# Starting a mixture of experts from seven of ten row tiles: six full expert tiles ahead of the last row tile

## What is computed

```python
x = x + _L0_gnn_ref(_layernorm(x), batch0, edge_index, W)      # attention over edges, 8 heads of 64
x = x + _L0_ffn_ref(_layernorm(x)[None], ...)[0]               # 8 experts, 2 for each node
x = x + _L1_gnn_ref(_layernorm(x), ..., src, dst)              # aggregate, project, layernorm, gelu
x = x + _L1_ffn_ref(_layernorm(x)[None], ...)[0]               # 6 experts, 1 for each node

# _L0_ffn_ref, for a node xf and its two best experts by xf @ gate_w:
h1 = rmsnorm(gelu(xf @ w1[e]), n1[e])
h2 = rmsnorm(gelu(h1 @ w2[e]), n2[e])
out = sum over the two of softmax(logit) * ((h2 + h1) @ w3[e])
```

## Time and profile before

| | us |
|---|---|
| median of 3 runs (lowest, highest) | 937.22 (934.82, 939.62) |
| the profiled execution's own time | 939.32 |
| its span in the trace | 937.6 |
| TensorE busy, share of the span | 842.7, 90% |
| VectorE busy | 572.0, 61% |
| ScalarE busy | 367.8, 39% |
| GpSimd busy | 221.4, 24% |

### The profile page before, as it was taken

How to read it: one execution, slowest core, us unless ns; L and a number is a source line. 1 busy time by engine, 2 the same in 40 slices (tenths; PEclk the granted TensorE clock), 3 DMA queues, 4 the chain that set the end, 5 groups by cost and what they waited for, 6 DMA issues and landing times.

```text
span 937.6 us, 15975 instructions
## 1 busy us (share of the span) xinstructions
PE 842.7 (90%) x5064; PEld 568.4 (61%) x5064; DVE 572.0 (61%) x1871; ACT 367.8 (39%) x674; POOL 221.4 (24%) x425
## 2 busy tenths in 40 slices
PE   6999999999999999999996399999829999983996
PEld 3456565367777777777775277777514444862674
DVE  6489999267778878887773245555524509674121
ACT  1234444366666566656662133434200021331331
POOL 4100000000012201220122322222156404773443
PEclk9999999999999999999998599999959999975999
DMA  9817867894011322014109545553123540254450
GB/s 251 305 39 203 203 194 197 188 302 119 28 51 51 100 59 77 24 50 179 53 24 326 161 121 156 157 171 105 61 83 89 128 144 27 102 187 102 152 178 27
DMA packets 86980, 121.27 MB, mean 129 GB/s; under 512 B 40270, under 2 KB 49646, under 8 KB 86638
## 3 DMA queue, kind: packets, MB, share of 16 engines
q1 hardware_dynamic: 73293, 102.08, 37.3%
q0 software_dynamic: 13600, 18.11, 6.7%
HBM read 65.78 MB, written 57.08 MB: 131 GB/s over the span
## 4 chain that ended last, share of the span: by engine, by line
PE 75%; DVE 11%; issue 5%; DMA 4%; ACT 2%; POOL 2%; SPq 0%; DVEq 0%; POOLq 0%; ACTq 0%
PE ps L715 18%; PE ps L608 10%; PE ps L637 10%; PE ps L779 9%; PE ps L619 8%; PE ps L498 4%; PE ps L804 4%; PE ps L722 4%; DVE R_B L1547 3%; DVE R_B L1546 2%; PE ps L503 2%; DVE R_A L1648 1%; PE ps L448 1%; PE ps L674 1%; DVE R_B L1542 1%
## 5 line engine op out<-in xcount | busy, mean ns | idle before, releaser
L715 PE MATMUL ps<-R_B,R_A 128*128 x612 | 187.4, 448 | 3.0 <-ACT R_A L1181 1.1
L715 PEld LDWEIGHTS ps<-R_B,R_A 128*128 128x128 f32 x612 | 112.9, 196 | 35.3 <-issue 24.8
L1026 ACT ACTIVATE R_A<-R_A,neg_max 125x1250 f32<-125x1250 f32 x80 | 106.6, 1333 | 56.6 <-DVE neg_max L1648 56.6
L1648 DVE CUSTOM_DVE_ANT_0 R_A<-ps,R_B,neg_max 125x417 f32<-125x417 f32 (+1 forms) x160 | 97.6, 648 | 29.0 <-PE ps L608 29.0
L608 PE MATMUL ps<-R_B 64*125 64x417 f32 (+1 forms) x480 | 106.5, 544 | 1.6 <-ACT XN L968 1.5
L637 PEld LDWEIGHTS ps<-R_W,XN 125*64 125x64 f32 x1600 | 85.3, 136 | 23.9 <-issue 23.8
L619 PE MATMUL ps<-ident,R_A 125*125 125x125 f32 x800 | 98.6, 278 | 0.0
L619 PEld LDWEIGHTS ps<-ident,R_A 125*125 125x125 f32 x800 | 94.9, 188 | 1.5 <-DVE R_W L1655 0.7
L637 PE MATMUL ps<-R_W,XN 125*64 125x125 f32 x1600 | 94.7, 272 | 0.8 <-DVE counted L1702 0.8
L1033 ACT ACTIVATE R_W<-ps 125x500 f32<-125x500 f32 x120 | 66.1, 585 | 51.1 <-PE ps L619 51.1
L1547 DVE TENSOR_SCALAR R_B<-R_B 125x418 bf16<-125x418 uint16 x200 | 76.8, 384 | 0.0
(11 more groups left out here) (238 smaller groups left out, 1134.8 us busy)
## 6 DMA issues: line engine op xcount, KB each, us to landing
slots_d<-R_B SPq DMA_DIRECT2D x9, 2322.0 KB, 12.1
R_B<-in_L_ffn_w_dram SPq DMA_DIRECT2D x28, 512.0 KB, 6.9
R_A<-slots_d SPq DMA_DIRECT2D x27, 256.0 KB, 2.9
slots_d<-R_A SPq DMA_DIRECT2D x27, 256.0 KB, 2.3
counts_d<-R_A SPq DMA_DIRECT2D x10, 546.9 KB
logs_d<-R_B SPq DMA_DIRECT2D x10, 546.9 KB
R_B<-logs_d SPq DMA_DIRECT2D x10, 546.9 KB
R_B<-counts_d SPq DMA_DIRECT2D x10, 546.9 KB
```

What stands on the lines that cost most here:

```text
L715: ins = pe.matmul(bank(b, TM, width), lhs[:, c * TM:c * TM + TM], flat[:, bass.ds(e * (n * width) + c * width, width)], start=c == 0, stop ...
L1026: act.activation(SC[u % 2][h], SC[u % 2][h], ACT.Exp, bias=neg_max[:, 2 * (u % 2) + h:2 * (u % 2) + h + 1], scale=-1.0, accum_out=den[:, 2 ...
L1648: dve.tensor_tensor_reduce(SC[u % 2][h][:, a:z], bank(2 * h + g % 2, P, z - a), LNB[i % 2][:, a:z], -1.0, least if t else 3.0e38, ALU.add, ...
```

## The change

The first six expert tiles (EARLY_TILES) are taken from the full tiles that the first seven row tiles (EARLY_ROWS) already fill; there are always six. Their counts are taken out at u = 36 (take_out_counts), and DVE works out owners and bases of these six tiles at the ends of u = 36, 37 and 38 (early_counts, early_owners, early_done; early_owners gives the first slot_made). SP loads the rows of tiles 0 to 2 when unit 38's weights are turned. The weights and norm vectors are loaded one by one, as attention lets go of the buffer beneath each; for that the queries lie by row tile, and XR and the routing's small tiles have moved. TensorE ends its attention loop at u = 40, and the output turn of unit 39 and the turn, logits and ranks of row tile 9 are written out by hand between the steps of tiles 0 to 3; the same on ACT, DVE and POOL. The counts of all rows are then taken out behind first_product(3). DVE makes of them the rest: rest_counts before second_squares(2) (the second slot_made with its first operation, for which third_product(1) waits), rest_owners in step 4 behind second_norm(2), rest_bases behind first_norm(4) (the third slot_made). SP waits for the third slot_made and all scatters before it loads the rows of tile 5, and turn_tile(6) and first_squares(6) wait for it too. The reloads of step 3 and later move four steps on. The gates come after the expert loop, and POOL's inverse degrees behind the root of row tile 8.

```diff
+EARLY_TILES, EARLY_ROWS = 6, 7
+assert K0 * P * EARLY_ROWS - E0 * (TM - 1) > (EARLY_TILES - 1) * TM
...
-        QT = R_B[:, 0:5000].rearrange("p (j n) -> p j n", j=4)
+        QT = R_B[:, 0:5000].rearrange("p (i j n) -> p i j n", i=T, j=4)
...
-        XR = [R_A[0:P, 5000 + WIDE * k:5000 + WIDE * k + WIDE] for k in range(3)]
+        XR = [R_B[0:P, 13056:13056 + WIDE], R_W[0:P, 5250:5250 + WIDE], R_B[0:P, 13572:13572 + WIDE]]
```

On SyncE:

```diff
-            sp.wait_ge(S("s_made"), 6 * UNITS)
...
-            sp.wait_ge(S("z_made"), 6 * UNITS)
...
-            sp.wait_ge(S("o_made"), UNITS)
...
+            for e in range(3):
+                load_w1e(e)
+            load_logs(9)
+            sp.wait_ge(S("s_made"), 6 * 9 * PAIRS)
+            load_w1e(3)
+            sp.wait_ge(S("z_made"), 6 * 9 * PAIRS)
+            load_w2e(4)
+            load_w2e(5)
+            sp.wait_ge(S("s_made"), 6 * (9 * PAIRS + 1))
+            load_w1e(5)
+            sp.wait_ge(S("s_made"), 6 * (9 * PAIRS + 2))
+            load_w1e(6)
+            sp.wait_ge(S("s_made"), 6 * (9 * PAIRS + 3))
+            load_w1e(7)
+            load_w2e(0)
             sp.wait_ge(S("slot_made"), 1)
             for k in range(3):
-                sp.wait_ge(rows_out[k], 16 * K0 * len(range(k, T, 3)))
+                sp.wait_ge(rows_out[k], 16 * K0 * len(range(k, EARLY_ROWS, 3)))
+            sp.wait_ge(S("p_turned"), BLOCKS * (UNITS - 1))
+            for t in range(3):
+                load_rows0(t)
+            sp.wait_ge(S("s_made"), 6 * UNITS)
+            load_w1e(4)
+            sp.wait_ge(S("o_made"), UNITS - 1)
+            load_norm(L0_ffn_n1, N1B, S("nrm_in"))
+            sp.wait_ge(S("z_made"), 6 * UNITS)
+            for e in (1, 2, 3, 6, 7):
+                load_w2e(e)
+            sp.wait_ge(S("o_made"), UNITS)
+            load_norm(L0_ffn_n2, N2B, S("gam_in"))
...
-            for t in range(MT0 + 2):
+            for t in range(3, MT0 + 2):
+                if t == EARLY_TILES - 1:
+                    sp.wait_ge(S("slot_made"), 3)
+                    for k in range(3):
+                        sp.wait_ge(rows_out[k], 16 * K0 * len(range(k, T, 3)))
                 if t < MT0:
                     load_rows0(t)
```

On TensorE (in the attention loop, the wait of a product, and behind the loop):

```diff
+            def take_out_counts(k):
+
+                pe.matmul(bank(7, 1, 8, 144), ident[0:126, 125:126], counted[:, k, :], start=True, stop=True,
+                          skip_group_check=True).then_inc(S("count_made"), 1)
...
-            for u in range(UNITS - PAIRS + RANKS_AT + 1):
+            for u in range(UNITS + 1):
...
+                    if tile_at(u, RANKS_AT) == EARLY_ROWS:
+                        take_out_counts(EARLY_ROWS % 2)
...
             def third_product(t):
+                if t == 1:
+                    pe.wait_ge(S("slot_made"), 2)
...
             turn_tile(0)
+            turn_output(UNITS - 1)
+            first_product(0)
+            turn_tile(1)
+            turn_first(0)
+            first_product(1)
+            turn_normed_row(T - 1)
+            turn_tile(2)
+            second_product(0)
+            output_bank_free(UNITS)
+            route_tile(T - 1)
+            turn_first(1)
+            first_product(2)
+            turn_second(0)
+            turn_tile(3)
+            rank_tile(T - 1)
+            second_product(1)
+            third_product(0)
+            turn_first(2)
+            first_product(3)
+            pe.wait_ge(S("rank_taken"), T)
+            take_out_counts(T % 2)
+            turn_second(1)
+            turn_tile(4)
+            second_product(2)
+            third_product(1)
+            for t in range(4, MT0 + 2):
```

On ScalarE:

```diff
-            act.wait_ge(S("gate_step"), 1)
-            act.activation(gates[:, 0, :], gates[:, 0, :], ACT.Exp).then_inc(S("gate_exp"), 1)
...
             move_tile(0)
...
+            first_gelu(0)
+            move_tile(1)
+            move_first(0)
+            first_gelu(1)
+            move_normed_row(T - 1)
+            move_tile(2)
+            second_gelu(0)
+            for t in range(2, MT0 + 2):
...
+            act.wait_ge(S("gate_step"), 1)
+            act.activation(gates[:, 0, :], gates[:, 0, :], ACT.Exp).then_inc(S("gate_exp"), 1)
```

On GpSimd:

```diff
+            for i in range(T - 1):
                 rstd_tile(S("ln_stat"), T + i + 1, i, None, S("ln_rstd"))
+                if i == T - 2:
+                    inverse_degrees()
                 masks_of(i)
                 slots_for(i)
...
+            inverse_rms(0, S("ss_made"), 1, S("rms_made"))
+            inverse_rms(0, S("ss_made"), 2, S("rms_made"))
+            inverse_rms(1, S("ss2_made"), 1, S("rms2_made"))
+            masks_of(T - 1)
+            inverse_rms(0, S("ss_made"), 3, S("rms_made"))
+            inverse_rms(1, S("ss2_made"), 2, S("rms2_made"))
+            slots_for(T - 1)
+            pool.wait_ge(S("count_made"), 2)
```

On VectorE, the bookkeeping and its places (early_counts at the end of step 36, early_owners of 37, early_done of 38):

```diff
+            def early_counts():
+                link(dve.tensor_scalar(cnt_i[0:1, :], cnt_i[0:1, :], 7, None, ALU.logical_shift_right))
+                link(dve.tensor_copy(full, cnt_i[0:1, :]))
+                link(dve.scalar_tensor_tensor(filled, iota8[0:1, :], -float(CAP // TM), full, ALU.mult, ALU.add))
+                link(dve.tensor_tensor_scan(ahead, ones_row, filled, 0.0, ALU.mult, ALU.add))
+                link(dve.tensor_scalar(step_of, filled, -1.0, float(CAP // TM), ALU.mult, ALU.add))
+            def early_owners():
+                tiles = EARLY_TILES
+                of, first = owner_f[:, 0:tiles], base_f[:, 0:tiles]
+                link(dve.tensor_tensor(early_owner, iotaT[:, 0:tiles].unsqueeze(2).to_broadcast([1, tiles, 8]),
+                                       cnt[0:1, 2:3, :].to_broadcast([1, tiles, 8]), ALU.is_ge))
+                link(dve.tensor_reduce(of, early_owner, X_AXIS, ALU.add))
+                link(dve.tensor_copy(owner_i[:, 0:tiles], of))
+                link(dve.tensor_tensor(early_owner, early_owner, cnt[0:1, 3:4, :].to_broadcast([1, tiles, 8]), ALU.mult))
+                link(dve.tensor_reduce(first, early_owner, X_AXIS, ALU.add))
+                link(dve.tensor_tensor(first, first, iotaT[:, 0:tiles], ALU.add))
+                dve.tensor_scalar(base_i[:, 0:tiles], first, float(TM), None, ALU.mult).then_inc(S("slot_made"), 1)
+            def early_done():
+                link(dve.tensor_scalar(ahead, ahead, float(EARLY_TILES), None, ALU.min))
+                link(dve.tensor_copy(taken[:, 0:1], ahead[:, 0:1]))
+                link(dve.tensor_tensor(taken[:, 1:8], ahead[:, 1:8], ahead[:, 0:7], ALU.subtract))
+            def rest_counts():
+                dve.wait_ge(S("count_made"), 2)
+                dve.tensor_scalar(cnt_i[0:1, :], bank(7, 1, 8, 144), float(TM - 1), None, ALU.add)\
+                   .then_inc(S("slot_made"), 1)
+                dve.wait_ge(S("slot_made"), 2)
+                link(dve.tensor_scalar(cnt_i[0:1, :], cnt_i[0:1, :], 7, None, ALU.logical_shift_right))
+                link(dve.tensor_copy(full, cnt_i[0:1, :]))
+                link(dve.scalar_tensor_tensor(filled, iota8[0:1, :], -float(CAP // TM), full, ALU.mult, ALU.add))
+                link(dve.tensor_scalar(step_of, filled, -1.0, float(CAP // TM), ALU.mult, ALU.add))
+                link(dve.tensor_tensor(filled, filled, taken, ALU.subtract))
+                link(dve.tensor_tensor_scan(ahead, ones_row, filled, 0.0, ALU.mult, ALU.add))
+                link(dve.tensor_tensor(step_of[:, 0:7], step_of[:, 0:7], taken[:, 1:8], ALU.add))
+            rest = MT0 - EARLY_TILES
+            rest_owner, rest_of = owner[:, 0:rest, :], owner_f[:, EARLY_TILES:MT0]
+            rest_first = base_f[:, EARLY_TILES:MT0]
+            def rest_owners():
+                link(dve.tensor_tensor(rest_owner, iotaT[:, 0:rest].unsqueeze(2).to_broadcast([1, rest, 8]),
+                                       cnt[0:1, 2:3, :].to_broadcast([1, rest, 8]), ALU.is_ge))
+                link(dve.tensor_reduce(rest_of, rest_owner, X_AXIS, ALU.add))
+                link(dve.tensor_scalar(rest_of, rest_of, float(E0 - 1), None, ALU.min))
+                link(dve.tensor_copy(owner_i[:, EARLY_TILES:MT0], rest_of))
+            def rest_bases():
+                link(dve.tensor_tensor(rest_owner, rest_owner, cnt[0:1, 3:4, :].to_broadcast([1, rest, 8]), ALU.mult))
+                link(dve.tensor_reduce(rest_first, rest_owner, X_AXIS, ALU.add))
+                link(dve.scalar_tensor_tensor(rest_first, iotaT[:, 0:rest], taken[:, 0:1], rest_first, ALU.add, ALU.add))
+                dve.tensor_scalar(base_i[:, EARLY_TILES:MT0], rest_first, float(TM), None, ALU.mult)\
+                   .then_inc(S("slot_made"), 1)
...
+            first_squares(0)
+            first_norm(0)
+            first_squares(1)
+            first_norm(1)
+            second_squares(0)
+            take_logits(T - 1)
+            pick_two(T - 1)
+            second_norm(0)
+            first_squares(2)
+            first_norm(2)
+            second_squares(1)
+            take_ranks(T - 1)
```

(17 more changed lines are left out.)

134 lines of the change are left out of this document (74 added, 60 removed).

## The result

The changed kernel takes 924.78 us (median of 4 runs, 924.32 to 925.81); the kernel before, beside it, 938.25 (4 runs, 934.82 to 939.62). The ratio is 0.9863 with a 95% interval of 0.9834 to 0.9893, which lies wholly under 1, so it is faster, by 13.5 us, where 11.1 had been forecast (926.1, range 918 to 932). The profiled execution took 924.32 us and its span is 922.5.

The account below looks back on a forecast made before the run. TensorE bounds the kernel, with a 23.5 us gap of hardly any work between attention and experts. Tile 5 turned 13.7 us earlier, less 2.55 for the low clock, gives 11.1 off 937.2: 926.1 us, range 918 to 932.

Parts of the forecast that it names:

- a new stall: TensorE idle 7.8 us before tile 5, whose load awaits bases and scatters; turned 35.75 after attention's last product ends (zero).
- the one for the first count operation: TensorE idle 1.95 us before third product 1, as POOL's scatters delay tile 3's root and so DVE's count.
- Attention: Early count on TensorE and sixteen tiny DVE operations in units 36 to 38 lengthen attention by 1.05 us.
- the low clock behind the stall: After 7.8 idle us before tile 5, the next 5.1 us do half their work: 2.55 us lost.
- The norm vectors: Loads asked for at -4.1 and later, first needed at 5.4 and 12; costed at nothing, upper bound 2.4 us late.
- The two added table loads: Exp between two uses of Gelu on ACT adds two loads of 1.28 us, covered by waits; nothing lost.
- Weights loaded early go out on an otherwise quiet queue: SP's early weight loads during attention cost nothing, since only later loads are queued behind SP's waits.
- no-stall: Rival: tile 5 turned at 27.95 without a long wait, clock held; gain 21.5 us, 915.7; chance 0.07 for the whole.
- The early fall of the clock: Rival: clock falls in the 2.05 us idle before tile 0's norm, costing half of 5.1 us: 928.7; shared chance 0.22.
- late vectors: Rival: norm vectors land late and cost 2.4 us, 928.5; 931 with an early clock fall; shared chance 0.22.
- The slower rival: Clock stays low from 5.9 through the filled stretch; tile 5 comes 18 us later, 944; chance 0.04.
- the price that the prediction put on them: By the skill's HAM section, the two small stalls before tile 5 would each cost 2.5 us more, giving 931.

Follow-up runs that it names:

- the second experiment: Changed kernel with tile 3's inverse root put first on POOL, ahead of row tile 9's slots and two scatters: 924.32 us, ratio 0.9858 to the kernel before.
- the filled wait: Changed kernel with 32 extra matmuls that nobody reads ahead of tile 5's turn on TensorE: 924.63 us, ratio 0.9854 to the kernel before.
- the late owners: Changed kernel with the early tiles' owner operations at the end of unit 38 instead of 37: 926.5 us, ratio 0.9858 to the kernel before.
- the count first: Changed kernel with DVE's eight count operations ahead of tile 3's norm instead of behind it: 925.96 us, ratio 0.9858 to the kernel before.
- the edits together: Changed kernel with SP's wait at tile 6, owners in unit 38, counts before tile 3's norm, and remaining owners and bases earlier: 917.47 us, ratio 0.976.
- The third experiment: Changed kernel with all eight first-weight loads moved back behind the last scores: 931.31 us, ratio 0.9935 to the kernel before.
- the wait at tile 6: Changed kernel with SP's wait for remaining bases and scatters one tile later, ahead of tile 6's load: 918.48 us, ratio 0.9797 to the kernel before.

## Why the prediction was right

**Where the time came from.** As forecast, the gap between attention and experts filled with the first tiles, and a new stall stood in front of tile 5. The tile came at zero + 35.37; forecast were 35.75. The wait there was 7.65 us (7.8), the one for the first count operation 2.42 (1.95), the one for tile 0's norm 2.13 (2.05). The chain over VectorE, GpSimd and SyncE, each link priced from a row of the kernel before, held to 0.65 us in every place, and the second experiment bears out the link that was least plain, the inverse root behind the scatters. Some of the closeness is luck, for misses cancelled. TensorE's stretch of queued work began at zero + 6.49 (5.9 forecast) but took 12.80 us up to the count and not 13.75; the last base came at zero + 31.47 (32.1), but from there to tile 5's turn it took 3.90 us and not 3.65.

**Attention.** 1.05 us was the cost forecast. The ranks that stand in unit 36 begin at 472.38 in the changed kernel and at 473.18 in the kernel before, and zero is 505.25 and 505.18, so the stretch grew from 32.00 to 32.87: 0.87 us. Of that 0.65 is the wait in unit 38 (0.81 us, formerly 0.16), which moving the owners took away. The early count itself is 0.20. The changed kernel, and then the one before, TensorE in order of time:

```profile
472.38 0.39 PE L719 MATMUL ps<-counted,before 126*126 126x8 f32 x2
```

```profile
473.18 0.39 PE L681 MATMUL ps<-counted,before 126*126 126x8 f32 x2
```

**The clock.** 2.55 us were forecast for the low clock behind the stall; the experts ended 2.08 later than tile 5's lead would have them, and the filled wait gives 2.10. The term was half a microsecond too high, because the clock was back 4.2 us after work resumed and not 5.1.

**The total.** 11.1 us were forecast; the medians differ by 13.5, the profiled executions by 15.0 (939.32 and 924.32). In the profiles tile 5 is 15.04 earlier, where the forecast had 13.7. Of these 1.4 us, 0.38 come from the shorter chain, 0.18 from attention's cost and 0.80 from an attention that started earlier in that execution, which the change has no part in. With the clock's 2.08 the experts end 12.96 us earlier. The other 2.1 of the profiles' 15 us lie in the stages behind them, from the last third product's start to the end of the span (256.5 us, not 258.65), and such a difference also exists between executions whose later stages are alike: in the nine profiles of the changed kernel and its variants it is 256.4 to 258.6 us, with a mean of 257.25. That is 1.4 under the one profile of the kernel before, which is not enough to say whether the change shortens these stages. Between the medians of the two kernels, what is left over the forecast is 2.4 us, with an interval of the ratio that is itself 5.5 us wide; it is not settled beyond that.

**What was costed at nothing.** The norm vectors were asked for at 501.2 and 505.8. The second landed 8.4 us later, at 514.2; the trace has no landing of the first, which took 7.1 us with the late owners, 4.8 with the count first and 7.6 with the edits together. TensorE's wait for tile 0's norm was 2.13 us, and VectorE's norm itself began behind GpSimd's root; the forecast's 2.05 has no late vector in it. The two added table loads on ScalarE take 1.28 us each and are covered: TensorE's wait ahead of the aggregation is 16.92 us, 17.51 before, and behind the second of the loads (757.30) ScalarE still waits 5.67 us for VectorE. ScalarE in order of time at the first of the two:

```profile
665.87 1.28 ACT L1188 ACT_TABLE_LOAD   x1
667.16 0.21 ACT L1188 ACTIVATE gates<-gates 125x10 f32<-125x10 f32 x1
```

The load begins 0.02 us behind the activation ahead of it (665.47 + 0.38), and the exponential 0.01 us behind the load. The Trainium skill, page "ScalarE: Activation LUTs", section on what ACT_TABLE_LOAD costs, makes about 2.7 us of 1.28 for the load and 1.38 for a drain. The load agrees; no gap of 1.38 us stands on either side of it here, and the measurement decides.

**Where it was too short.** "Weights loaded early go out on an otherwise quiet queue" counted as a cost of nothing, and the sum began with the first product unhindered. It does not say that without them the first product would stand. The third experiment shows 6.8 us resting on it. The forecast came out since the weights were there, but a reader would have taken the gain for that of order alone.

**The rivals.** The stall is real, so no-stall is out as a forecast; as an experiment, one line takes it away, and 918.48 stands against the 915.7 reckoned for it. Of that, 0.97 us are left in front of tile 6, and the fall of the clock behind the count's wait made the chain 0.9 longer; the rest was not taken apart. The early fall of the clock was given 0.22 together with late vectors. It did not happen in the changed kernel's profile, but did in four of the profiles of its variants: behind the count's wait in three (the wait at tile 6, the filled wait, the late owners), in the first products in one (the count first). Behind the count it cost less than the 2.6 us reckoned. The wait for the bases took up what TensorE alone lost, and what was left is what the chain grew by: from the first count operation to the last base 9.04, 9.09 and 9.08 us in these three, 8.18 in the changed kernel. The slower rival, the clock low through the whole filled stretch, is excluded here by 1.00 from 505 to 537. It is real in a kernel that lets the clock fall first: with row tile 9 put first it was at 0.50 from 512 to 528, and the gain was down to 0.2%. The Trainium skill, "TensorE: Matmul & The Clock Gate", section on HAM oscillation, has bursts of matmuls start slow each time behind a long DMA wait. This case agrees: each of the six waits of 6.7 to 7.8 us in front of tile 5 was followed by work at 0.50. The section's case does not hold waits near 2 us, so the price that the prediction put on them does not follow from it. Here such waits went either way.

## What to carry to other kernels

When work is moved ahead into a gap, ask what it then waits for: here a single wait stood one tile ahead of where the data required it, and moving that line gave 6 us on top of the 13.5 of the whole rework. Ask too what the old order let happen in good time: weights loaded early carried half of this gain. Follow the small operations of the side engines link by link, since those, and not the big matmuls, set when the next load may go. Judge small edits in front of a long wait by what they do to the chain that ends it, for the wait swallows all that only the waiting engine gains. An edit that delays a load also delays every load behind it in the same queue, as the late owners did with the second weights.

## What had not been expected of the hardware

- The clock's fall after idle time varies. It came 3.1 us after the last matmul in the kernel before (505.55 + 0.37 to 509.0), 2.1 at its experts' end (680.93 to the 0.53 of 683 to 684), 5.0 in the changed kernel (532.98 to 538.0), 1.1 with the root first (531.85 to 533.0, the matmuls just before having waited 1.75), and once at 515.4, when TensorE had been working again for 1.5 us after a wait of 1.84. Of five executions with a wait of 2.40 to 2.42 us for the count, two kept the full clock and three lost it; of seven with one of 1.84 to 2.13 us for tile 0's norm, one lost it.
- Eight loads of 512 KB, issued in one row at attention's end, needed 17 us, 246 GB/s for them, with the transfer engines busy for 0.99 of the time at 326 GB/s in all.
- A 128 by 128 matmul with its weight load, in a row of 32 with alternating weights, took 0.22 us at full clock from start to start; the rows show 0.39 for its two records, as their modelled ends overlap the next.
